# Pieces of the identity turned into an unread bank in nine waits of TensorE

## The chip, the cores and the metric

One Trainium2 chip, one of its cores. The metric is device time in microseconds for one execution of the whole program, lower is better. A profiled execution also gives the span from the first to the last instruction, and the clock that TensorE was granted, as a share of its full speed: 1.00 is 2.4 GHz, 0.50 is 1.2 GHz.

## The reference

A transformer block on x of 16 batches x 224 tokens x 512 channels, with 16 heads of 32 channels, and a context of 750 tokens per batch. Cut to what matters:

```python
shift_a, scale_a, gate_a, shift_m, scale_m, gate_m = split(silu(c) @ W_mod + b_mod, 6)
q, k, v = heads(modulate(ln(x), shift_a, scale_a) @ W_qkv + b_qkv)
x = x + gate_a * (softmax(q @ k.T * scale) @ v @ W_proj + b_proj)      # self attention
q_c = heads(ln(x) @ W_qc + b_qc)
k_c, v_c = heads(ln(context) @ W_kvc + b_kvc)
x = x + softmax(q_c @ k_c.T * scale) @ v_c @ W_cproj + b_cproj         # cross attention
h = gelu(modulate(ln(x), shift_m, scale_m) @ W_mlp1 + b_mlp1)          # MLP
x = x + gate_m * (h @ W_mlp2 + b_mlp2)
```

All in float32. The kernel splits most operands into a high and a low part and makes a product of three matmuls (the helper `product`, lines 72 to 74).

## The kernel before, in words

There are three phases: self attention (to about 767 us), cross attention (from 771 to about 1912 us) and the MLP (to the end). The places where one phase runs into the next are called seams. Self attention ends with a barrier of all engines (`clear`, lines 98 and 99); cross attention and the MLP are one program.

Self and cross attention go through the batches in *bodies*, one for a batch, of 16 *steps* (`h`), one for a head. TensorE's order is written out by hand in each body: `score` makes the scores of the next head (L599 in self, L1779 in cross), VectorE takes their maximum (`row_max`, L908; L1965 and L1967 in cross), after every fourth head TensorE turns the maxima into a row (`turn_maxima`, L616; L1767), VectorE splits that row (`split_maxima`, L915; L2012) and SyncE's queue copies it into the stacked queries (`place_maxima`, L437; L1669). Six steps later `score_t` makes the same scores with keys on the partitions and the maxima subtracted (L628; L1793), and ScalarE takes the exponential (L1160; L2138). Every four heads `pv` multiplies by the values (L645; in the last cross body `product_parts`, L1835) and `sums` adds up the probabilities (L652) that GpSimd has added in pairs (L1295). VectorE divides (`normalize`: reciprocal L922, product L925; L2019, L2025).

In between, `fill` puts projections of other batches into the steps (L72 to L74). In the last bodies there is less left to fill in. What the change touches or what follows on it there:

- Self attention's last full body (b.c = 15) runs from about 664 us. Step 2 has `score` of head 3, then `pv` and `sums` of the batch before. Step 3 fills in query channels ("c"), then turns maxima. Steps 4 and 5 turn x after its layernorm (`turn_y`, L562), of which the second waits for VectorE's `low_y` (L865). Step 6 has `pv` of the batch before, step 7 a fill of channels and then `turn_maxima`, which needs `row_max` of head 7. VectorE has the context's statistics (`stats_context`, L876) ahead of that maximum.
- The end of self attention is a last fill ("c", 1, 1), then the barrier.
- Cross attention begins with `score` of batch 0. SyncE's queue begins after the barrier too: it stores the last queries, loads and stacks (L1654, L1661), and then places the first maxima (L1669), for which `score_t` of step 6 waits.
- Cross attention's last body (b.c = 15) runs from about 1823 us. In step 6 the last products of the batch before let SyncE's queue load the first attention outputs (`load_first_o`, L1684, into mlp_o_raw). ScalarE splits them from step 8 on (`first_high_o`, L2113), between its exponentials. Steps 11 to 14 have the output projection of four tiles (`first_cproj`, L72 to L74 with mlp_wcp); that of tile 3 waits until VectorE has read tile 1 out of the same bank (`first_residual`, L1978).

A wait on a semaphore stops all that TensorE has behind it. The bank a step writes to is 512 words wide; the new function writes to columns 448 to 511, which nobody reads in the banks it is given.

Of the kernel before, what the change touches and what calls it, by code (L numbers as in the profile page):

```python
# [21 lines left out]
B, N, H = 16, 224, 512  # L22
# [54 lines left out]
def keep_warm(pe, bank, ident, count):  # L77

    for _ in range(count):
        pe.transpose(bank[:, 0:P], ident[:], ident[:])  # L80


def alloc(nc, ctx, phase):
# [80 lines left out]
def self_phase(nc, x, cond_t, w_mod, b_mod, w_qkv, b_qkv_t, w_proj, b_proj, w_qc, b_qc_t, gates, x1, qc, mod_t,  # L164
# [3 lines left out]
    with ExitStack() as ctx:  # L168
# [240 lines left out]
        def late_group(b, h, att, prv):  # L409

            if h % HPG != (LAG + HPG) % HPG:
                return []
            g = (h - LAG - HPG) // HPG
            if g >= 0:
                return [(b, g)] if att else []
            return [(b.plus(-1), g + KC)] if prv else []
# [139 lines left out]
        def _(pe):  # L556
# [185 lines left out]
            def body(b, att, nxt, prv, old):  # L742
                for h in range(NH):
                    for o, l in late(b, h, att, prv):
                        score_t(o, l)
                    work = fills(b, h, "kqvpc")
                    for f in work[0:1]:
                        fill(b, *f)
                    if h % HPG == HPG - 1 and att:
                        turn_maxima(b, h // HPG, old)  # L750
                    if h < NH - 1 and att:
                        score(b, h + 1)
                    if h == NH - 1 and nxt:
                        score(b.plus(1), 0)
                    for f in work[1:]:
                        fill(b, *f)

                    if seam_step(b, h) in V_AT:
                        cross_v(V_AT[seam_step(b, h)])
                    if seam_step(b, h) in K_AT:  # L760
                        cross_k(K_AT[seam_step(b, h)])
                    if b.c == 1 and h in (13, 14):
                        pe.wait_ge(proj_done, h - 12)
                        modulation_rows(h - 9)
                    for o, g in late_group(b, h, att, prv):
                        pv(o, g)
                        sums(o, g)
                    for _, c, _, o in fills(b, h, ("tx",)):
                        turn_x(b, c, o)
                    for t in TILES_AT.get(seam_step(b, h), ()):  # L770
                        turn_context(0, t)
                    for _, c, _, o in fills(b, h, ("ty",)):
                        turn_y(b, c, o, att)
                    if b.c == 0 and h == NH - 1:
                        pe.wait_ge(v_done, Batch(1).n(2, 2))
                        modulation_rows(3)
                    if b.c == 1 and h == 15:
                        pe.wait_ge(mlp_rows, 2)
                        turn_rows(pj_ps[1], lambda n, k: wm_mlp[0:B, n, 0, k * P:(k + 1) * P], mod_turned)
# [31 lines left out]
            turn_context(1, 5)  # L811
            fill(end, "c", 1, 0, last)
            fill(end, "c", 1, 1, last)

        @block.vector
        def _(dve):
# [620 lines left out]
def cross_phase(nc, ctx_in_dram, qc, o_dram, wkv, c_in, seam, pieces, ident, neg_half, eps, sems, banks, lead):  # L1437
# [291 lines left out]
    def tensor(pe):  # L1729
# [136 lines left out]
        def body(b, att, nxt, prv):  # L1866
            a = b.plus(1)
            for h in range(NH):
# [8 lines left out]
                for f, o in fill_at(b, h, "kv"):  # L1877
                    fill_(o, f, (0,))
                if cproj_due is not None:
                    first_cproj(cproj_due, (0,))  # L1880
                for o, l in late(b, h, att, prv):
                    score_t(o, l, 1)
                if h < NH - 1 and att:
                    score(b, h + 1, 0)
                if h == NH - 1 and nxt:
# [6 lines left out]
                    product_parts(*MID_PARTS[step])  # L1892
                if h % HPG == HPG - 1 and att:
                    turn_maxima(b, h // HPG)
                for o, l in late(b, h, att, prv):
                    score_t(o, l, 2)
                for u in (1, 2):
# [875 lines left out]
```

## Time and profile before

| | |
|---|---|
| median of 3 runs | 2616.03 us |
| lowest and highest | 2615.39, 2621.15 us |
| the profiled execution's own time | 2619.34 us |
| its span | 2617.5 us |
| mean granted clock | 0.991 |
| TensorE matmuls busy | 2578.0 us, 98% of the span |
| VectorE, ScalarE, GpSimd busy | 1694.1, 1126.6, 1275.6 us |

The profiled execution is one run of the same program. Its time has 1.8 us outside the span. TensorE's busy time counts a matmul from its start to its modelled end, about 0.2 us behind the moment at which the next one can start.

### The profile page before, as it was taken

Reading aid. Unit: us, or ns where it says so; the run is one execution under the profiler, and the core shown is the slowest. Engines: PE = TensorE matmul, PEld = TensorE weight load, DVE = VectorE, ACT = ScalarE, POOL = GpSimd, SP = SyncE. Lnnn points to the kernel's source line nnn. Section 1 sums busy time; section 2 is a strip of 40 time slices with the busy share of each in tenths; the row PEclk is TensorE's granted clock in tenths of the full one; section 3 lists DMA queues with packets and bytes.
Section 4 is the critical chain, followed back from the end, with each engine's and each line's share of the span. In section 5 each row is a group of like instructions: output and inputs, shape, how many; then the busy total and the mean of one; then the engine's idle time right before and its main releaser. Section 6 shows DMA issues by size and latency. Waiting matters only on the chain.

```text
span 2617.5 us, 50236 instructions
## 1 busy us (share of the span) xinstructions
PE 2578.0 (98%) x18696; PEld 2133.6 (82%) x18696; DVE 1694.1 (65%) x3399; ACT 1126.6 (43%) x2192; POOL 1275.6 (49%) x1426
## 2 busy tenths in 40 slices
PE   8999999999999999999999999999899999999999
PEld 6688888888788888888888888887678888888887
DVE  6677777777757777777777777776764444444442
ACT  4354454444535555555555555554552221212111
POOL 1445455454436777777777777775421121220230
PEclk9999999999899999999999999999899999999999
DMA  8454545555454444444444444434521111111110
GB/s 225 128 136 125 135 120 130 129 129 132 137 148 111 115 115 112 113 114 112 117 114 116 119 113 115 121 90 102 153 94 45 37 44 34 45 49 37 45 53 17
DMA packets 193045, 269.89 MB, mean 103 GB/s; under 512 B 34788, under 2 KB 112612, under 8 KB 192788
## 3 DMA queue, kind: packets, MB, share of 16 engines
q1 hardware_dynamic: 187116, 254.16, 36.9%
q0 software_dynamic: 3264, 7.92, 0.9%
q10 hardware_dynamic: 2424, 4.61, 0.7%
q8 instruction: 150, 2.46, 0.4%
q14 instruction: 91, 0.75, 0.1%
HBM read 111.11 MB, written 36.77 MB: 56 GB/s over the span
## 4 chain that ended last, share of the span: by engine, by line
PE 69%; DVE 1%; issue 0%; DMA 0%; ACT 0%; SPq 0%; DVEq 0%; ACTq 0%
PE late_tr_ps L1793 7%; PE late_sc_ps L1779 7%; PE late_or_ps L1806 5%; PE late_even_ps L72 5%; PE late_sc_ps L72 5%; PE late_even_ps L73 5%; PE late_even_ps L74 5%; PE late_sc_ps L74 5%; PE late_sc_ps L73 5%; PE late_odd_ps L72 3%; PE late_odd_ps L74 3%; PE late_odd_ps L73 3%; PE late_tr_ps L74 2%; PE late_tr_ps L72 2%; PE late_tr_ps L73 2%; PE late_odd_ps L1740 1%
## 5 line engine op out<-in xcount | busy, mean ns | idle before, releaser
L2138 ACT ACTIVATE cross_prT<-late_tr_ps 125x448 f32<-125x448 f32 x759 | 403.0, 544 | 273.5 <-PE late_tr_ps L1793 264.6
L1965 DVE TENSOR_REDUCE cross_parts<-late_sc_ps 112x1 f32<-112x500 f32 x512 | 335.5, 663 | 221.8 <-PE late_sc_ps L1779 220.7
L2211 POOL TENSOR_TENSOR cross_part<-cross_prT 125x448 f32<-125x448 f32 x232 | 271.2, 1169 | 214.6 <-ACT cross_prT L2138 176.9
L1295 POOL TENSOR_TENSOR self_psum<-self_prT 112x224 f32<-112x224 f32 x256 | 179.0, 699 | 328.3 <-ACT self_prT L1160 319.5
L1793 PE MATMUL late_tr_ps<-cross_qst,cross_kst 98*125 98x224 f32 x1536 | 309.5, 284 | 5.4 <-ACT cross_prT L2138 4.4
L1793 PEld LDWEIGHTS late_tr_ps<-cross_qst,cross_kst 98*125 98x125 f32 x1536 | 255.3, 188 | 55.8 <-ACT cross_prT L2138 16.5
L2613 ACT ACTIVATE mlp_hv<-late_sc_ps,mlp_b 128x512 f32<-128x512 f32 x112 | 77.0, 687 | 511.5 <-PE late_sc_ps L74 497.1
L2213 POOL TENSOR_TENSOR cross_part<-cross_part,cross_prT 125x448 f32<-125x448 f32 x232 | 268.5, 1157 | 18.2
L1779 PE MATMUL late_sc_ps<-cross_kst,cross_qst 96*112 96x500 f32 (+1 forms) x1024 | 262.2, 337 | 5.2 <-PEq L99 3.3
L2527 DVE CAST mlp_hT_h<-mlp_hv 128x512 fp32r<-128x512 f32 x112 | 55.9, 499 | 301.8 <-ACT mlp_hv L2613 301.8
L1160 ACT ACTIVATE self_prT<-self_st_ps 112x448 f32<-112x448 f32 x256 | 138.4, 541 | 167.6 <-PE self_st_ps L628 166.4
L1779 PEld LDWEIGHTS late_sc_ps<-cross_kst,cross_qst 96*112 96x112 f32 x1024 | 165.2, 179 | 20.1 <-issue 3.5
L908 DVE TENSOR_REDUCE self_nmax<-self_sc_ps 112x2 f32<-112x448 f32 x256 | 154.5, 614 | 33.3 <-PE self_sc_ps L599 33.2
L72 PE MATMUL late_sc_ps<-mlp_xT_l,mlp_w_h 128*128 128x512 f32 x448 | 175.8, 393 | 0.0
L74 PE MATMUL late_sc_ps<-mlp_xT_h,mlp_w_h 128*128 128x512 f32 x448 | 175.2, 391 | 0.0
L73 PE MATMUL late_sc_ps<-mlp_xT_h,mlp_w_l 128*128 128x512 f32 x448 | 175.0, 391 | 0.0
L1967 DVE TENSOR_REDUCE cross_parts<-late_sc_ps 112x2 f32<-112x500 f32 x256 | 170.2, 665 | 0.0
L2215 POOL TENSOR_TENSOR cross_psum<-cross_part 125x224 f32<-125x224 f32 x232 | 155.6, 671 | 18.2
L1806 PE MATMUL late_or_ps<-cross_prT,cross_vt 125*32 125x224 f32 x2784 | 143.7, 354 | 0.0
L72 PE MATMUL self_pj_ps<-self_xT_l,self_wqkv_h 128*128 128x224 f32 x512 | 140.6, 275 | 2.4 <-DVE self_wm_gates L1009 1.4
L74 PE MATMUL self_pj_ps<-self_xT_h,self_wqkv_h 128*128 128x224 f32 x512 | 140.6, 275 | 0.0
L73 PE MATMUL self_pj_ps<-self_xT_h,self_wqkv_l 128*128 128x224 f32 x512 | 140.3, 274 | 0.0
(343 smaller groups left out, 6870.9 us busy)
## 6 DMA issues: line engine op xcount, KB each, us to landing
cross_kst<-cross_nat_h SPq DMA_DIRECT2D x508, 93.8 KB, 2.2
cross_kst<-cross_nat_l SPq DMA_DIRECT2D x254, 93.8 KB, 2.2
cross_qst<-qc SPq DMA_DIRECT2D x192, 112.0 KB, 2.5
cross_c_in<-in_context SPq DMA_DIRECT2D x78, 224.0 KB
self_kst<-self_nat_h SPq DMA_DIRECT2D x128, 112.0 KB, 2.3
self_qst<-self_natq_h SPq DMA_DIRECT2D x128, 112.0 KB, 3.0
self_x_in<-in_x SPq DMA_DIRECT2D x16, 448.0 KB, 3.8
self_kst<-self_nat_l SPq DMA_DIRECT2D x64, 112.0 KB, 2.2
```

The source lines that it names most:

```text
L72: pe.matmul(out, lhs[0], rhs[1], start=first, stop=False)
L73: pe.matmul(out, lhs[1], rhs[0], start=False, stop=False)
L74: return pe.matmul(out, lhs[0], rhs[0], start=False, stop=last)
L1295: pool.tensor_tensor(psum[:, j], prT[:, j, 0], prT[:, j, 1], ALU.add).then_inc(p_summed, 1)
L1779: last = pe.matmul(sc_ps[u][0:QN, at:at + cn], qst[g][0:TERMS * HD, j, t * QN:(t + 1) * QN], kst[g][j][0:TERMS * HD, c0:c0 + cn], start=Tr ...
L1793: last = pe.matmul(bank(h, c)[0:SN, m * N:(m + 1) * N], kst[g][j][:, kt * SN:(kt + 1) * SN], qst[g][:, j, :], start=True, stop=True)
L1806: last = pe.matmul(or_ps[HD * j:HD * j + HD, 0:N], vt[b.par][:, kt, h * HD:h * HD + HD], prT[:, slot(h), kt], start=kt == 0, stop=kt == ST ...
L1965: dve.tensor_reduce(parts[:, g % 2, j, u, 0:1], sc_ps[u][0:QN, 0:SHALF[0]], AX_X, ALU.max, negate=True).then_inc(maxed, 1)
L1967: dve.tensor_reduce(parts[:, g % 2, j, :, 1], sc_ps[u][0:QN, 0:QT * SHALF[1]].rearrange("p (t k) -> p t k", t=QT), AX_X, ALU.max, negate=T ...
L2138: act.activation(probabilities(b, h)[:, 2 * c:2 * c + 2], bank(h, c)[0:SN, 0:2 * N].rearrange("p (k t) -> p k t", k=2), ACT.Exp).then_inc( ...
L2211: pool.tensor_tensor(part[:], prT[:, j, 0:2], prT[:, j, 2:4], ALU.add).then_inc(pre_summed, 1)
L2213: pool.tensor_tensor(part[:], part[:], prT[:, j, 4:6], ALU.add).then_inc(pre_summed, 1)
```

## The change

A function `stay_busy` transposes half of the identity (64 of its rows, 128 columns wide, against a 64 x 64 identity) into columns 448 to 511 of a bank, so and so many times. It is called in nine places; four of them have a wait of their own ahead of it, so that the bank is not being read by another engine.

```diff
+def stay_busy(pe, bank, ident, count):
+    for _ in range(count):
+        pe.transpose(bank[:, 448:512], ident[0:64, :], ident[0:64, 0:64])
...  self attention, body (b.c = 15)
                         turn_maxima(b, h // HPG, old)
+                    if b.c == B - 1 and h == 2:
+                        pe.wait_ge(m_row, b.n(KC, 0))
+                        stay_busy(pe, tx_ps, ident, 16)
                     if h < NH - 1 and att:
                         score(b, h + 1)
...
                     for o, g in late_group(b, h, att, prv):
+                        if b.c == B - 1 and h == 6:
+                            stay_busy(pe, pj_ps[1], ident, 16)
                         pv(o, g)
+                        if b.c == B - 1 and h == 2:
+                            stay_busy(pe, tx_ps, ident, 18)
                         sums(o, g)
+                    if b.c == B - 1 and h == 5:
+                        pe.wait_ge(c_l, Batch(B - 4).n(2, 2))
+                        stay_busy(pe, pj_ps[1], ident, 10)
...  end of self attention
             fill(end, "c", 1, 1, last)
+            stay_busy(pe, tx_ps, ident, 40)
...  cross attention, body (step = h in the last body)
                 if cproj_due is not None:
+                    if step == 14:
+                        pe.wait_ge(maxed, b.n(NH * 3, (NH - 1) * 3 - 2))
+                        stay_busy(pe, sc_ps[0], ident, 28)
                     first_cproj(cproj_due, (0,))
                 for o, l in late(b, h, att, prv):
                     score_t(o, l, 1)
+                if step == 5:
+                    pe.wait_ge(*turn_bank_free(b, 1))
+                    stay_busy(pe, odd_ps, ident, 12)
                 if h < NH - 1 and att:
                     score(b, h + 1, 0)
...
+                if step in (8, 9):
+                    pe.wait_ge(m_row, b.n(KC, 2))
+                    stay_busy(pe, odd_ps, ident, {8: 12, 9: 28}[step])
                 for o, l in late(b, h, att, prv):
                     score_t(o, l, 2)
```

In all 180 transposes. Nothing is removed or reordered.

## Rows read from the trace of the kernel before

**Rows 1.** The page: TensorE's granted clock in 40 slices, in tenths.

```profile
PEclk9999999999899999999999999999899999999999
```

**Rows 2.** Stretches (us): busy PE, PEld, DVE, ACT, POOL; granted clock, DMA share, GB/s.

```profile
671.33:678.16 6.83, 5.93 (x34) 5.19 (x34) 1.75 (x6) 2.88 (x6) 2.32 (x4) 0.50 0.93 224
681.57:688.40 6.83, 6.62 (x44) 5.21 (x45) 6.67 (x21) 1.46 (x3) 2.03 (x3) 0.50 0.64 193
770.32:777.15 6.83, 6.30 (x20) 5.90 (x21) 2.72 (x6) 0.52 (x1) 3.59 (x6) 0.50 1.04 299
1842.11:1845.52 3.41, 3.41 (x36) 1.75 (x38) 1.63 (x3) 0.98 (x2) 2.14 (x5) 0.50 0.84 233
1855.76:1862.59 6.83, 5.05 (x38) 3.46 (x42) 4.65 (x8) 3.72 (x7) 1.54 (x2) 0.50 0.60 181
1883.07:1886.48 3.41, 3.41 (x11) 2.67 (x9) 3.38 (x6) 0.54 (x1) 3.03 (x3) 0.50 0.01 2
1844.00:1855.50 11.50, 10.61 (x119) 6.72 (x111) 6.12 (x12) 5.54 (x11) 5.26 (x5) 0.93 1.05 273
```

**Rows 3.** Timeline of PE, transposes of 16 columns (start, us, engine, idle in brackets).

```profile
17.56 0.66 PE L739 MATMUL self_st_ps<-shared_ident,self_bm 16*128 16x16 f32 x8
```

**Rows 4.** Timeline of PE, self attention's last full body.

```profile
669.49 0.46 PE L599 MATMUL self_sc_ps<-self_kst,self_qst 96*112 96x224 f32 x2 [1.09 <-DVE self_nmax L908]
...
672.23 0.98 PE L652 MATMUL self_or_ps<-self_psum,self_ones 112*32 112x224 f32 x8 [1.39 <-POOL self_psum L1295]
...
676.21 0.39 PE L616 MATMUL self_tx_ps<-shared_ident,self_nmax 112*8 112x112 f32 x1
...
679.72 0.61 PE L562 MATMUL self_tx_ps<-shared_ident,self_x_res 112*128 112x112 f32 x4 [0.59 <-DVE self_yT_l L865]
...
681.77 1.72 PE L645 MATMUL self_or_ps<-self_prT,self_vt 112*32 112x224 f32 x16 [1.03 <-DVE self_ou L925]
...
687.37 0.35 PE L616 MATMUL self_tx_ps<-shared_ident,self_nmax 112*8 112x112 f32 x1
...
704.86 0.62 PE L701 MATMUL self_pj_ps<-shared_ident,cross_c_in 125*128 125x125 f32 x4 [1.54 <-DVE self_y L856]
```

**Rows 5.** Timeline of DVE, same stretch, and its last work before the barrier.

```profile
676.63 0.26 DVE L915 CAST self_mrow_h<-self_tx_ps 8x112 fp32r<-8x112 f32 x1 [4.97 <-PE self_tx_ps L616]
...
686.72 0.59 DVE L908 TENSOR_REDUCE self_nmax<-self_sc_ps 112x2 f32<-112x448 f32 x1
...
768.41 0.81 DVE L846 SCALAR_TENSOR_TENSOR self_natq_l<-self_pj_ps,self_bqcs,self_natq_h 128x224 fp32r<-128x224 f32 x2 [1.63 <-ACT self_natq_h L1146]
```

**Rows 6.** Timeline of PE, the first seam and cross attention's step 6.

```profile
770.85 1.56 PE L1779 MATMUL late_sc_ps<-cross_kst,cross_qst 96*112 96x500 f32 x4 [3.30 <-PEq L99]
...
792.10 0.60 PE L1793 MATMUL late_tr_ps<-cross_qst,cross_kst 98*125 98x224 f32 x4
```

**Rows 7.** Timeline of SyncE's queue and, last row, PE: maxima placed by DMA.

```profile
789.47 0.65 SPq L1669 DMA_DIRECT2D cross_qst<-cross_mrow_l  x1
...
68.49 0.67 SPq L437 DMA_DIRECT2D self_qst<-self_mrow_l  x1
...
70.30 0.50 PE L628 MATMUL self_st_ps<-self_qst,self_kst 98*112 98x224 f32 x2 [0.17 <-DMA self_qst<-self_mrow_l]
```

**Rows 8.** Timeline of PE, four waits of cross attention's last body.

```profile
1839.99 0.48 PE L1779 MATMUL late_sc_ps<-cross_kst,cross_qst 96*112 96x500 f32 x1 [0.86 <-DVE cross_parts L1965]
...
1853.51 0.48 PE L1793 MATMUL late_tr_ps<-cross_qst,cross_kst 98*125 98x224 f32 x2 [0.76 <-ACT cross_prT L2138]
...
1857.54 0.76 PE L1793 MATMUL late_tr_ps<-cross_qst,cross_kst 98*125 98x224 f32 x2 [1.91 <-ACT cross_prT L2138]
...
1881.80 0.50 PE L72 MATMUL late_odd_ps<-mlp_wcp_l,mlp_xT_l 128*128 128x512 f32 x1 [1.78 <-DVE mlp_x L1978]
```

**Rows 9.** The chain that ended last, 1847 to 1857 us (start, us, what).

```profile
1847.54 8.71 DMA mlp_o_raw<-o_cross
```

**Rows 10.** Timeline of DVE ahead of the last wait.

```profile
1880.48 0.67 DVE L1965 TENSOR_REDUCE cross_parts<-late_sc_ps 112x1 f32<-112x500 f32 x1
```

## The prediction

> **What bounds the kernel now.** I read the page first. TensorE's matmuls are busy for 98% of the span (the table above), and its granted clock has two dips, in slices 11 and 29, which are the two seams [rows 1]. So the kernel is bound by TensorE, and what can be won in the seams is idle time and slow clock. The windows by stretch then show the dips as six stretches in which the clock stood at its lower level, 0.50, together 34.1 us (6.83 four times, 3.41 twice), with TensorE busy for 5.93, 6.62, 6.30, 3.41, 5.05 and 3.41 = 30.7 us of it [rows 2]. At full clock that work would take half, so 15.4 us is the most that a better clock can return. I call the stretches A to F in their order. Ahead of each the timeline shows TensorE idle: 1.09 and 1.39 us ahead of or into A, 0.59 and 1.03 ahead of B [rows 4], 3.30 ahead of C [rows 6], 0.86 ahead of D, 0.76 and the begin of 1.91 ahead of E, 1.78 ahead of F [rows 8]. The nine calls stand in just these waits. The reader should look next at who would be late if TensorE were faster after them: VectorE, SyncE's queue and a DMA, stretch by stretch.
>
> **What a transpose costs.** The trace has none of 64 columns. Eight of 16 columns take 0.66 us together with the last one's latency of about 0.2, so about 0.065 us each [rows 3]; four of 112 columns take 0.61, so about 0.11 each at the most [rows 4]. Those are the bounds. If the cost goes with the columns, 64 would take 0.06, and the small ones show a floor of 0.065, so I take 0.065; at the lower clock twice the 0.06, about 0.11.
>
> **Do they fit the waits?** At 0.065: 16 are 1.04 us against 1.09 idle, 18 are 1.17 against 1.39, 10 are 0.65 against 0.59, 16 are 1.04 against 1.03 [rows 4]; 12 are 0.78 against 0.86, 12 are 0.78 against 0.76, 28 are 1.82 against 1.91 [rows 8]. A further 0.2 us of matmul latency lies ahead of each idle time and hides the small excess. These seven cost nothing; without that cover the 112 transposes would be 7.3 us. The waits put ahead of three of them ask for rows of maxima, channels or a bank that were done long before, so nothing queues behind them. Two do not fit.
>
> The 40 at the end of self attention are 2.6 us. TensorE's last product ends at 767.55 (770.85 less 3.30), its stream 0.2 us earlier, so TensorE would end at about 770.1 with the latency, while VectorE, now the last to come to the barrier, ends at 769.22 [rows 5, 6]. The barrier, and with it all engines, comes 0.8 us later (0.6 at 0.06 each, 2.6 at 0.11).
>
> The 28 in step 14 must first wait for `row_max` of head 14, which VectorE runs from 1880.48 to 1881.15 [rows 10], late, just ahead of the read that releases TensorE at 1881.80 [rows 8]. So they run from 1881.15 to about 1883.0, and the projection behind them starts 1.2 us later than now (1.0 at 0.06 each, 2.4 at 0.11).
>
> **What the full clock returns, if the falls go away.**
> - A. From 672.23 to the turned maxima at 676.21 TensorE works without a wait [rows 4]; 4.0 us become 2.0. From there VectorE is busy without a break from 676.63 to past 687 (6.67 of 6.83 us in B's row) [rows 2, 5], so everything behind it moves by these 2.0 and no more. Return 2.0, at most 3.0.
> - B. TensorE now reaches the next turned maxima at 687.37, and VectorE ends the maximum that it needs at 687.31 [rows 4, 5]. A faster TensorE only waits there. Only the last 1.0 us of B returns 0.5. At most 3.3.
> - C. TensorE would come to step 6, now at 792.10 [rows 6], up to 3.1 us earlier. But `score_t` needs the maxima, whose DMA SyncE's queue issues at 789.47 after a row of copies that starts at the barrier; the same kind of DMA elsewhere released TensorE 1.8 us after its issue (68.49 to 70.30) [rows 7]. So it can start at 791.3, and with the later barrier at 792.1. Delay and clock cancel: 0.0, between 1.8 lost (a barrier 2.6 later) and 0.2 won (0.6 later).
> - D. The products of step 6 stand in the chain, but what follows is a DMA of 8.71 us [rows 9], in a stretch in which the DMA engines are full (share 1.05 from 1844 to 1855.5) [rows 2]. Issued earlier it lands hardly earlier, so the 1.7 us are waited away in step 9. I take 0, at most 1.7.
> - E. It follows that landing; 5.05 us busy give up to 2.5, ScalarE's exponentials between them take a little: 2.3.
> - F. All TensorE: 1.7 returned, 1.2 spent on the late transposes: 0.5.
>
> The sum is 2.0 + 0.5 + 0.0 + 0.0 + 2.3 + 0.5 = 5.3 us. The profiled execution's own time is 2619.34 (span 2617.5 and 1.8 around it), so 2614.0. It was 3.3 us above the median of 2616.03. A run near the median may have lacked one of the low stretches, and what it lacks can't be taken out of it; so I don't subtract the whole 5.3 there. I forecast 2613.5 for the median, 2.5 us or 0.1% better. About 0.2%, 5.2 us, is what a measurement of this kernel can tell from no change, so this counts as no change.
>
> **A rule that speaks against it.** TensorE idles 1.54 us at 704.86 between transposes [rows 4], and the clock stays at 1.00 there (the next low stretch is C [rows 2]), while the idle 1.78 us ahead of F, among matmuls, is followed by 0.50 [rows 2, 8]. The Trainium skill, TensorE: Matmul & The Clock Gate, Part 4 (PE-mode transpose), says that a transpose "doesn't count as PE-busy the same way". The two waits lean against that rule, but do not settle it; by the rule the sum would be that of the third rival below.
>
> **Rivals.**
> 1. *It all passes through.* VectorE, the queue and the DMA make room, since their work starts earlier too: 15.4 less 0.8 and 1.2 is 13.4 us, 2606. Against it stand the three meeting points above, of which that in B is within 0.1 us.
> 2. *The waits that open drop the clock again*, the slower side. At full clock TensorE comes to the maxima of step 7 2.6 us before VectorE (5.6 us of work from 681.77 become 2.9, then VectorE), and 2.3 us early to step 6 of cross attention (3.1 less 0.8). Neither wait has transposes, and idle times of 1.8 and 1.9 us were enough for a fall before. In step 9 D's 1.5 us lengthen a wait whose 28 transposes stay the same. A fall costs half of 3.4 or 6.8 us, so 1.7 to 3.4, twice, and E's 2.3 are not won: 2614.0 + 3.4 to 6.8 + 2.3 = 2619.7 to 2623.1. It is decided where the idle rest passes about 1.8 us, and by how the wait falls in time.
> 3. *Transposes don't hold the clock.* All six low stretches stay, the 28 in step 9 run mostly at 0.11 each and overrun by 0.9 us, with 0.8 for the barrier and 1.2 in step 14: 2.9 us more, 2622.
>
> **How the numbers follow.** The forecast 0.45 (its own range 2610 to 2617.5), the first rival 0.20, the second 0.20, the third 0.10, something between them 0.05. Under 2610.8 lie the first rival and a fifth of the forecast: faster 0.30. Over 2621.3 lie half of the second and most of the third, less what a median near the lower runs takes off: slower 0.15. No change 0.55. The range that leaves out 2 in 10 is 2607 to 2621.5.
>
> **What would show it.** In the profile after: spacing of the new transposes near 0.065 us; the clock at 1.00 where A, C and F stood; the first matmul of cross attention 3.4 to 3.5 us after the last product of self attention becomes 4.2 to 4.4; an idle time of some 2.6 us at the turned maxima of step 7 and of some 2 us at the `score_t` of step 6, with or without low clock behind; the DMA into mlp_o_raw landing at the same distance from the seam; the projection of tile 3 about 1.9 us behind `row_max` of head 14. The prediction is wrong if VectorE or SyncE's queue turn out to have slack, or if the new waits drop the clock in each run.

## The result, and the profile after

The changed kernel takes 2620.57 us in the median of 13 runs (2616.95 to 2623.29), the kernel before 2615.39 us in the median of 13 (2612.52 to 2621.15) beside it. The ratio is 1.0015 with a 95% interval of 1.0008 to 1.0022, so it is slower, by 0.15%. The forecast was 2613.5, faster by 0.1%; the time lies in the range from 2607 to 2621.5, the direction does not.

The two profiled executions hide this: before's own time is 2619.34 us, after's 2619.05. They were unlike draws, one 3 to 4 us above its median, the other 1.5 below it. So these profiles can't be subtracted from each other; they can be followed place by place.

The windows of the profile after, in the columns of [rows 2]. The first, third and fourth rows lie where A, C and D stood, the others are its own low stretches and the time ahead of the last:

```profile
669.00:675.83 6.83, 6.49 (x73) 4.99 (x71) 2.99 (x9) 4.13 (x8) 4.21 (x6) 1.00 0.72 184
680.26:687.09 6.83, 6.83 (x48) 5.25 (x47) 5.69 (x19) 0.54 (x1) 2.98 (x4) 0.50 0.47 152
770.32:777.15 6.83, 6.75 (x39) 6.50 (x40) 5.42 (x10) 1.15 (x2) 4.88 (x8) 1.00 0.83 247
1842.11:1845.52 3.41, 3.41 (x65) 2.21 (x61) 1.43 (x3) 1.57 (x3) 1.07 (x2) 1.00 1.03 263
1854.45:1861.28 6.83, 6.06 (x42) 3.83 (x46) 3.82 (x6) 2.84 (x6) 2.42 (x2) 0.50 0.82 246
1878.35:1881.76 3.41, 2.23 (x30) 2.12 (x30) 3.33 (x8) 2.11 (x4) 1.09 (x3) 1.00 0.01 4
1881.76:1885.17 3.41, 3.41 (x10) 2.74 (x10) 1.62 (x3) 0.54 (x1) 2.70 (x3) 0.50 0.00 0
```

Three stretches are gone (A, C, D) and three remain in new places, at 680.26 for B, 1854.45 for E, 1881.76 for F: 17.1 us of half clock instead of 34.1. Had these 17 us returned half of themselves, the span would be some 8 us shorter. It is 0.2 us shorter.

The timeline of PE of the changed kernel, lines with L86 being the new transposes (start, us, engine; idle in brackets):

```profile
669.03 0.47 PE L605 MATMUL self_sc_ps<-self_kst,self_qst 96*112 96x224 f32 x2
...
673.92 0.26 PE L622 MATMUL self_tx_ps<-shared_ident,self_nmax 112*8 112x112 f32 x1
...
676.72 0.84 PE L86 MATMUL self_pj_ps<-shared_ident 64*128 64x64 f32 x10
...
679.28 1.30 PE L86 MATMUL self_pj_ps<-shared_ident 64*128 64x64 f32 x16
680.51 1.72 PE L651 MATMUL self_or_ps<-self_prT,self_vt 112*32 112x224 f32 x16
...
685.98 0.39 PE L622 MATMUL self_tx_ps<-shared_ident,self_nmax 112*8 112x112 f32 x1
...
766.07 2.74 PE L86 MATMUL self_tx_ps<-shared_ident 64*128 64x64 f32 x40
770.40 0.91 PE L1796 MATMUL late_sc_ps<-cross_kst,cross_qst 96*112 96x500 f32 x4 [1.59 <-PEq L105]
...
790.16 0.67 PE L1810 MATMUL late_tr_ps<-cross_qst,cross_kst 98*125 98x224 f32 x4 [1.20 <-DMA cross_qst<-cross_mrow_l]
...
1837.95 0.48 PE L1796 MATMUL late_sc_ps<-cross_kst,cross_qst 96*112 96x500 f32 x1
...
1849.91 0.48 PE L1810 MATMUL late_tr_ps<-cross_qst,cross_kst 98*125 98x224 f32 x2
...
1851.91 1.98 PE L86 MATMUL late_odd_ps<-shared_ident 64*128 64x64 f32 x28
1854.78 0.76 PE L1810 MATMUL late_tr_ps<-cross_qst,cross_kst 98*125 98x224 f32 x2 [0.89 <-ACT cross_prT L2164]
...
1856.82 1.18 PE L1810 MATMUL late_tr_ps<-cross_qst,cross_kst 98*125 98x224 f32 x4 [0.45 <-DMA cross_qst<-cross_mrow_l]
...
1862.17 0.48 PE L1810 MATMUL late_tr_ps<-cross_qst,cross_kst 98*125 98x224 f32 x2
...
1879.57 1.98 PE L86 MATMUL late_sc_ps<-shared_ident 64*128 64x64 f32 x28 [1.18 <-DVE cross_parts L1991]
1881.48 0.57 PE L72 MATMUL late_odd_ps<-mlp_wcp_l,mlp_xT_l 128*128 128x512 f32 x1
```

Set each line against its twin of before. The difference of the two start times is how far after is ahead, and its steps are the ledger:

| place | before | after | ahead | step |
|---|---|---|---|---|
| scores ahead of A [rows 4] | 669.49 | 669.03 | 0.46 | |
| maxima turned, through A [rows 4] | 676.21 | 673.92 | 2.29 | +1.8 |
| maxima turned, through B [rows 4] | 687.37 | 685.98 | 1.39 | -0.9 |
| cross attention begins [rows 6] | 770.85 | 770.40 | 0.45 | -0.9 |
| `score_t`, step 6 [rows 6] | 792.10 | 790.16 | 1.94 | +1.5 |
| ahead of D [rows 8] | 1839.99 | 1837.95 | 2.04 | +0.1 |
| `score_t`, step 8, past D [rows 8] | 1853.51 | 1849.91 | 3.60 | +1.6 |
| `score_t`, step 9 [rows 8] | 1857.54 | 1854.78 | 2.76 | -0.8 |
| step 11, past E | 1863.81 | 1862.17 | 1.64 | -1.1 |
| projection of tile 3 [rows 8] | 1881.80 | 1881.48 | 0.32 | -1.3 |

In this pair of executions, what was won in A, the first seam and D (4.9 us) was lost in B, at the barrier, in step 9, E and step 14 (5.0 us). The experiments ask which of the two columns belongs to the change.

### The profile page after: what moved, and what is told of

Read it like the earlier page. It is cut to its first block, busy times and chain, and to the rows that moved or that the text cites. A ratio compares the mean times of both kernels' runs of the same rounds, so it can differ in the third digit from the quotient of the medians.

```text
span 2617.3 us, 50596 instructions
## 1 busy us (share of the span) xinstructions
PE 2583.7 (99%) x18876; PEld 2140.2 (82%) x18876; DVE 1694.0 (65%) x3399; ACT 1126.6 (43%) x2192; POOL 1276.2 (49%) x1426
## 4 chain that ended last, share of the span: by engine, by line
PE 68%; SPq 1%; DVE 1%; issue 0%; DMA 0%; ACT 0%; DVEq 0%
PE late_tr_ps L1810 7%; PE late_sc_ps L1796 6%; PE late_or_ps L1823 5%; PE late_sc_ps L72 5%; PE late_sc_ps L74 5%; PE late_sc_ps L73 5%; PE late_even_ps L72 5%; PE late_even_ps L73 5%; PE late_even_ps L74 5%; PE late_odd_ps L72 3%; PE late_odd_ps L74 3%; PE late_odd_ps L73 3%; PE late_tr_ps L74 2%; PE late_tr_ps L72 2%; PE late_tr_ps L73 2%; PE late_odd_ps L1757 1%
## 5 line engine op out<-in xcount | busy, mean ns | idle before, releaser
L2239 POOL TENSOR_TENSOR cross_part<-cross_part,cross_prT 125x448 f32<-125x448 f32 x232 | 268.7, 1158 | 18.2
L2241 POOL TENSOR_TENSOR cross_psum<-cross_part 125x224 f32<-125x224 f32 x232 | 155.5, 670 | 18.2
```

The costliest lines, as they stand in the source:

```text
L2239: pool.tensor_tensor(part[:], part[:], prT[:, j, 4:6], ALU.add).then_inc(pre_summed, 1)
```

## The experiments

Each kernel ran 11 times unless said otherwise, and the kernel before beside it. "Mean" is over these runs, the granted clock too. A mean clock below 1 is read as half clock: 0.9938 over 2615 us is 32 us of it.

### The kernel before, again

No edit.

> The kernel before once more, with no edit, so that the clock and span of each of its runs are seen. Theory 1 (the profiled execution is typical in its clock): the granted clock is 0.990 to 0.992 in most runs, the median lies at 2615 to 2616, and a new profile shows the same six stretches of half clock in the two seams, 37 us in all, within 0.2 us of their places. Theory 2 (the profiled execution of before, 3.3 us above its median, had more half clock than most): most runs show 0.993 or more, and the new profile lacks at least one of the six stretches; then part of what the change took away was not there to take.

Median 2617.15 us, ratio 1.0003 (0.9994 to 1.0013), clocks from 0.993 to 0.997. The profiled execution took 2613.39 us at 0.995. Its timeline has no low stretch at A or F, 3.41 us in place of B's 6.83, and 3.41 us more at 701.63, where the first profile has none; windows of it:

```profile
660.00:677.70 17.70, 12.45 (x104) 9.77 (x101) 13.19 (x29) 8.21 (x16) 8.08 (x11) 1.00 0.55 142
677.74:681.15 3.41, 3.41 (x31) 1.81 (x29) 3.41 (x7) 0.60 (x2) 0.66 (x1) 0.50 1.04 313
701.63:705.04 3.41, 3.41 (x31) 2.23 (x24) 2.94 (x6) 1.32 (x3) 3.25 (x3) 0.50 0.24 70
766.48:773.31 6.83, 5.61 (x18) 5.32 (x19) 2.61 (x5) 0.00 (x0) 3.06 (x5) 0.50 1.05 288
1838.27:1841.68 3.41, 3.41 (x27) 2.21 (x31) 2.23 (x4) 0.98 (x2) 2.65 (x6) 0.50 0.85 227
1851.92:1858.75 6.83, 6.83 (x51) 4.08 (x55) 4.93 (x9) 2.89 (x6) 2.99 (x3) 0.50 0.78 236
1880.00:1912.00 32.00, 29.59 (x344) 20.28 (x346) 20.70 (x51) 18.79 (x35) 6.84 (x10) 1.00 0.31 106
```

That is 23.9 us in the seams, where the first profile has 34.1. The same program has its low stretches for other lengths, and in part at other places, from one execution to the next. Theory 2 holds. Four profiles are of kernels that fill no wait at all (the two of before, and `waits_only` and `before_w_later` below). A and F are in one of them. B, C, D and E are in all four, B twice and C once at half length. Over the 149 runs of the kernel before that stood beside the experiments the clock goes from 0.990 to 0.998 with a mean of 0.9938; the profiled execution of the forecast had 0.991, and only six of the 149 are as low. The time goes with the clock: the 19 runs at 0.992 or less took 2619.5 us in the mean, the 43 at 0.993 2617.6, the 35 at 0.994 2615.9, and the 52 at 0.995 or more 2614.6.

### Parts of the change, alone

`self_body`, `end_40`, `steps_5_8_9` and `step_14` each keep one group of calls. As an example, the calls that `self_body` leaves out:

```diff
-            stay_busy(pe, tx_ps, ident, 40)
...
-                    if step == 14:
-                        pe.wait_ge(maxed, b.n(NH * 3, (NH - 1) * 3 - 2))
-                        stay_busy(pe, sc_ps[0], ident, 28)
...
-                if step == 5:
-                    pe.wait_ge(*turn_bank_free(b, 1))
-                    stay_busy(pe, odd_ps, ident, 12)
...
-                if step in (8, 9):
-                    pe.wait_ge(m_row, b.n(KC, 2))
-                    stay_busy(pe, odd_ps, ident, {8: 12, 9: 28}[step])
```

> Only the four calls in self attention's last full body (16, 18, 10 and 16 transposes), the other calls left out. Theory 1 (the sum of the forecast: the clock stays up where the waits are filled): 2.5 us under before, no half clock between 665 and 695. Theory 2 (what the profile of the changed kernel shows in this place is the rule: one fall of the two goes, the other stays, a clock period earlier): about 1 us under before, one stretch of 6.8 us that begins near 680.3, and stretch C at 770 unchanged. Theory 3 (the calls cost time in places that the profile doesn't show): 1 us or more over before, with the same clock as in theory 2.

> Only the 40 transposes at the end of self attention. Theory 1 (forecast: the barrier comes 0.8 us later, what stretch C returns is lost to the wait for m_in's maxima): 0.8 us over before, no half clock at 770. Theory 2 (stretch C's 1.6 us come back, and the wait for the maxima at step 6 takes 1.2 of them): 0.4 us under before to 0.4 over it. Theory 3 (the later barrier puts everything behind it at another place against the DMA queues): 2 us or more over before, in a profile whose cross bodies wait more often than before's.

> Only the calls of the last cross body's steps 5, 8 and 9 (12, 12 and 28 transposes). Theory 1 (forecast: stretch E goes and returns 2.3 us): 2.3 us under before, no half clock from 1850 to 1870. Theory 2 (the changed kernel's profile is the rule: the stretch of 3.4 at 1842 goes, the one of 6.8 stays a period earlier): within 0.5 us of before, one stretch of 6.8 us near 1854.5 to 1856. Theory 3 (no cover: the transposes' own time is on the path): 1 us or more over before.

> Only the 28 transposes of the last cross body's step 14. Theory 1 (they wait for the last heads' maxima and then take 1.98 us, where before's wait of 1.78 us was for mlp_x alone): about 1.4 us over before, a row of 28 transposes that starts after an idle time near 1.2 us, and the wait that before shows at this place lengthened from 1.78 to 3.2 us. Theory 2 (the loss of this place lies behind the wait as well, in head 15's exponentials, which come late): 2 us or more over before. Theory 3 (the clock that they hold pays for them): within 0.7 us of before, and no half clock behind 1880.

| | median us | ratio to before, interval | mean clock |
|---|---|---|---|
| `self_body` | 2616.76 | 1.0002 (0.9994 to 1.0011) | 0.9941 |
| `end_40` | 2618.61 | 1.0006 (0.9997 to 1.0015) | 0.9940 |
| `steps_5_8_9` | 2616.33 | 0.9995 (0.9986 to 1.0004) | 0.9955 |
| `step_14` | 2618.70 | 1.0004 (0.9996 to 1.0013) | 0.9930 |

No part is told from before by its time alone. `self_body` was to be 2.5 us under, and its interval, 1.6 us under to 2.9 over, rules that out. `steps_5_8_9` was to be 2.3 us under, and its interval, 3.7 us under to 1.0 over, does not. The latter's profile has what theory 2 said, a stretch of 6.83 us at 1856.01, and one of 3.41 at 1838.94 besides. `self_body` fits none of its three theories whole: its stretch begins where theory 2 has it, but there is none at 770, and its time is not below before's. The profiles say more, since a stretch between two fixed instructions can be read to 0.02 us.

*Self attention's last body.* From one turning of maxima to the next ([rows 4]: 676.21 to 687.37, 11.16 us) the 13 profiles without narrow transposes there (seven with empty waits, six with the wide pieces of the kernels below) took 11.11 to 11.16 us, and the six with them 12.06, 12.16, 12.55, 12.68, 12.89 and 13.92. The first of the two turnings settles stretch A: from the turning ahead of it to 676.21 before took 12.12 us, and all 18 others, with and without the calls, 10.3. Stretch A was in that one execution, and the 16 and 18 transposes of step 2 cost nothing. In the second half the low stretch of B is there at full length, 6.83 us, in all six with narrow transposes, in four of the seven with empty waits (twice at half length, once not at all), and in none of the six with wide pieces. (Of the 20 profiles `matmul_fill`, below, is left out here, since its fills overran the waits.)

Why the calls cost there is seen in two profiles with the same length of half clock in that half. `steps_5_8_9` has no transposes in this body; its window, and PE's timeline:

```profile
678.41:685.24 6.83, 6.53 (x42) 4.58 (x43) 6.68 (x14) 1.99 (x4) 0.66 (x1) 0.50 0.92 284
```

```profile
674.97 0.26 PE L622 MATMUL self_tx_ps<-shared_ident,self_nmax 112*8 112x112 f32 x1
...
680.73 1.72 PE L651 MATMUL self_or_ps<-self_prT,self_vt 112*32 112x224 f32 x16
...
686.09 0.26 PE L622 MATMUL self_tx_ps<-shared_ident,self_nmax 112*8 112x112 f32 x1 [0.17 <-DVE self_nmax L914]
```

VectorE is busy for 6.68 of 6.83 us, TensorE still waits 0.17 us for it at the end, and the 11.12 us are those of full clock: the waits that were left empty had absorbed 6.83 us of half clock. (`wide_transposes`, below, has no low clock there and takes 11.12 us too, with a wait of 1.18 us for VectorE at the end.) `self_body` has such a fall at 679.92, and filled waits:

```profile
679.86 1.95 PE L86 MATMUL self_pj_ps<-shared_ident 64*128 64x64 f32 x16
681.74 1.72 PE L651 MATMUL self_or_ps<-self_prT,self_vt 112*32 112x224 f32 x16
...
687.00 0.26 PE L622 MATMUL self_tx_ps<-shared_ident,self_nmax 112*8 112x112 f32 x1
```

The 16 take 1.88 us to the next start, 0.118 each, against 0.065 at full clock. The products begin 7.29 us after the first turning, against 5.76 in `steps_5_8_9`, and the next turning comes after 12.55 us with no wait ahead of it. A second thing goes into this stretch: TensorE waits there for the row of maxima that SyncE's queue copies (self_qst<-self_mrow_l), 0.56 to 0.75 us in the four shorter of the six, 1.06 us in that of 12.89 (`no_40_no_14`) and 2.17 us in that of 13.92 (`no_40_14_w_later`). With empty waits even 1.45 us of it, beside 3.41 us of half clock (`before_again`), left the 11.12 us as they were. So the upper end of the six is also that wait's, which filled waits no longer hide.

*The end of self attention.* From the end of the last product to cross attention's first matmul the changed kernel takes 770.40 less 766.13 = 4.27 us against 3.30 [rows 6]: 0.97 more. From there to the `score_t` of step 6, profiles without the 40 took 20.9 to 21.3 us with a fall of 6.8 us there, 19.9 to 20.2 with one of 3.4, and 19.2 in the one without a fall; the four with them took 19.8 to 20.0, with a fall of 3.4 in three of them. The six profiles in which no wait ahead of this place is filled and the 40 are left out average 20.7 us, the four with the 40 transposes 19.9. So the 40 cost 0.97 and give back about as much, 0.85, by few profiles. `end_40` has its stretch at 768.03, and its waits elsewhere are those of before, so its profile bears out theory 2; its median does not contradict theory 1.

*Step 14.* The row at 1879.57 above waits for a maximum (1.18 us), then 1.91 us go by before the projection starts, where before waited 1.78 us in all [rows 8]: 1.3 us. `step_14` shows the same two numbers, 1.18 and 2.08 us. The fall that the calls were to prevent came under them or right behind them in three of the four profiles with these calls (1881.76 in the changed kernel, 1879.71 in `step_14`, 1876.8 in `after_w_later`, below), and not in `after_again`. Of the 13 profiles with this wait empty four have it, within 1.4 us behind the projection's start: the first of before and three of the kernels with wide pieces in seven waits. Theory 1 holds for the place; the mean, 1.5 us over before, is not outside the interval.

### The changed kernel again, without its two costly places, and with its waits alone

`no_40_no_14` leaves out the 40 and the 28 of step 14. `waits_only` keeps the five added `wait_ge` (the description of the change counts four; its diff has five, and six of the nine calls stand behind one) and makes `stay_busy` empty.

> The changed kernel once more, on the chip of the three below. Theory 1 (the loss is the kernel's own: its clock is a little higher than before's, and its waits longer): 3 to 6 us over before, a mean granted clock of 0.994 to 0.995 against 0.9938 over 33 runs of before. Theory 2 (the first comparison drew an unlucky spread): within 2 us of before.

> The changed kernel without the 40 at the end of self attention and without the 28 of step 14. Theory 1 (these two are the loss: 1.0 and 1.4 us): 2.4 us or more under the changed kernel of this call, within 2 us of before. Theory 2 (the loss is that of waits for transfers, which take what the clock returns, wherever the calls are): within 1 us of the changed kernel.

> The changed kernel with its four added waits and without any transpose. Theory 1 (the time is in the transposes; the waits are for work that had come): as before, within 0.5 us, and a mean clock of 0.9935 as before. Theory 2 (the wait for the last heads' maxima itself delays mlp_o's product in step 14): 1 us or more over before, with the idle time of that place near 1.8 us or above.

`after_again`: median 2618.36 us in 12 runs, ratio 1.0004 (0.9996 to 1.0012), mean clock 0.9950. By its time this is theory 2, within 2 us of before, by its clock theory 1, and taken alone it is not told from before. Over all 25 runs of the changed kernel the mean is 2619.3 us at a clock of 0.9948, against 2616.4 at 0.9938 over the 149 of before; in the first measurement the means are 4.3 us apart, in the second 1.3. So the loss is nearer 3 us than 5, and it comes with a little less half clock (27 us instead of 32). `no_40_no_14`: 2616.31 us, ratio 0.9998 (0.9989 to 1.0006), 2 us under `after_again` in the median: near theory 1's 2.4. `waits_only`: 2617.22, ratio 1.0000 (0.9991 to 1.0009), clock 0.9939, an idle time of 1.83 us in step 14: the waits cost nothing, the transposes do.

### What is put into the waits

Three kernels keep the nine places and change the filling.

```diff
-    for _ in range(count):
-        pe.transpose(bank[:, 448:512], ident[0:64, :], ident[0:64, 0:64])
+    # matmul_fill
+    for _ in range(round(count * 0.6)):
+        pe.matmul(bank[:, 448:512], ident[0:64, :], ident[0:64, 0:64], start=True, stop=True)
+    # wide_transposes
+    for _ in range(round(count * 0.6)):
+        pe.transpose(bank[:, 384:512], ident[:], ident[:])
+    # wide_matmuls
+    for _ in range(round(count * 0.25)):
+        pe.matmul(bank[:, 384:512], ident[:], ident[:], start=True, stop=True)
```

> The changed kernel with plain matmuls of the same pieces in place of the transposes, 0.6 times as many because a plain fp32 matmul of 64 columns should take about 0.11 us, so the waits are filled for about as long. Theory 1 (transposes count for the clock as matmuls do): clocks and time as those of the changed kernel, within 0.0005 and 1.5 us. Theory 2 (transposes count for little: the array is idle through much of them): a mean clock above 0.9955, at most two stretches of half clock in the seams, and 1 to 3 us under the changed kernel.

> The nine waits filled with transposes of the whole 128x128 identity, 0.6 times as many (about 0.11 us each in keep_warm's burst at the start), so the same waits are filled for the same time and each transpose moves twice the columns. Theory 1 (the pieces of 64 columns are too small to count, wide ones count): mean clock 0.9955 or more, no stretch of 6.8 us begins between 679 and 681 and none near 1854 to 1859, and at least 1.5 us under the changed kernel's mean. Theory 2 (no transpose counts): mean clock 0.994 to 0.995, the stretch near 680.5 stays, time within 1.5 us of the changed kernel.

> The same waits filled with plain fp32 matmuls of the whole identity, a quarter as many (0.2 to 0.3 us each, worked out from the 0.24 us that one of 64 columns took). Theory 1 (plain matmuls count where transposes don't): mean clock 0.9955 or more and no half clock in the filled places, while the wide transposes show 0.995 or less. Theory 2 (what is put into the waits doesn't decide, since the waits at other places are enough for a fall): clock and time as the changed kernel's.

`matmul_fill` (5 runs): 2640.62 us, ratio 1.0086 (1.0073 to 1.01), clock 0.990. Its size was misjudged: a plain fp32 matmul of 64 columns took 0.24 us, not 0.11, so the fills overran their waits by some 20 us in all. It still shows the one thing that it was for. PE's timeline at the end of self attention, and windows of it:

```profile
770.34 6.47 PE L86 MATMUL self_tx_ps<-shared_ident 64*128 64x64 f32 x48
```

```profile
771.40:774.80 3.40, 3.40 (x33) 3.40 (x33) 0.67 (x2) 0.00 (x0) 0.00 (x0) 1.00 1.03 247
774.80:778.20 3.40, 2.01 (x10) 1.82 (x9) 0.00 (x0) 0.00 (x0) 0.00 (x0) 0.50 0.03 5
```

TensorE is busy from 770.34 to 776.81 without a break, all of it narrow plain matmuls, and the clock falls in the middle, at 774.8. So a busy row of narrow pieces did not hold the clock, and it is not the transposing.

Wide pieces mostly do hold it. `wide_transposes`: mean clock 0.9980, `wide_matmuls` 0.9976, 10 to 13 us of half clock left. In its profile `wide_transposes` has one low stretch in both seams:

```profile
660.00:800.00 140.00, 131.63 (x952) 113.86 (x951) 98.67 (x205) 65.69 (x127) 58.52 (x70) 1.00 0.50 138
1800.00:1854.00 54.00, 50.54 (x469) 37.15 (x468) 35.78 (x63) 26.30 (x52) 19.14 (x23) 1.00 0.59 152
1854.01:1860.84 6.83, 6.13 (x51) 3.47 (x53) 3.08 (x5) 2.13 (x4) 3.32 (x3) 0.50 0.77 228
1860.90:1912.00 51.10, 47.52 (x483) 35.05 (x476) 36.41 (x76) 28.93 (x54) 16.38 (x21) 1.00 0.31 103
```

Theory 1 of `wide_transposes` holds for the mean clock, and its mean time, 2615.7 us, is 3.6 us under the changed kernel's 2619.3; only the stretch at 1854.01 is against it. Theory 1 of `wide_matmuls`, by which plain matmuls count where transposes don't, is refuted, since both held the clock. Against the kernel before, the time is hardly better: 2616.03 us, ratio 0.9996 (0.9987 to 1.0005), and 2615.65, ratio 0.9996 (0.9988 to 1.0005). Twenty microseconds less half clock bought 1 us or less. (These pieces have more rows and more columns than the narrow ones; which of the two counts was not tried.)

Step 9 of `wide_transposes` shows where part of the rest went. Timelines of PE and ACT:

```profile
1853.60 0.48 PE L1810 MATMUL late_tr_ps<-cross_qst,cross_kst 98*125 98x224 f32 x2 [2.01 <-ACT cross_prT L2164]
...
1855.57 1.18 PE L1810 MATMUL late_tr_ps<-cross_qst,cross_kst 98*125 98x224 f32 x4 [0.70 <-DMA cross_qst<-cross_mrow_l]
```

```profile
1852.39 0.72 ACT L2139 ACTIVATE mlp_xT_l<-mlp_o_raw,mlp_bv 128x512 fp32r<-128x512 f32 x1 [3.72 <-DMA mlp_o_raw<-o_cross]
```

and the chain of waits:

```profile
1847.73 7.79 DMA cross_qst<-cross_mrow_l
```

There are two waits. In the longer one, 2.01 us, TensorE waits for ScalarE's exponentials, and ScalarE has stood 3.72 us ahead of them, in `first_high_o`, until the load of mlp_o_raw landed. The shorter, 0.70 us, is for the row of maxima of 3.5 KB, which took 7.79 us from SyncE's queue to its landing. In the changed kernel the two are 0.89 us (ScalarE waits 2.60 us for mlp_o_raw) and 0.45 us (a row of 6.53 us, issued at 1850.25, TensorE goes on at 1856.82). Ahead of the row are seven weight pieces and the four of mlp_o_raw, 256 KB each; ahead of mlp_o_raw are the seven pieces. The issues of mlp_o_raw, in `wide_matmuls`, where TensorE comes there earliest (SyncE's queue issues them at 1839.35, that of before at 1846.68, and the last landed 8.71 us after 1847.54 [rows 9]):

```profile
mlp_o_raw<-o_cross SPq DMA_DIRECT2D x4, 256.0 KB, 12.0
```

and in the kernel before, again:

```profile
mlp_o_raw<-o_cross SPq DMA_DIRECT2D x4, 256.0 KB, 6.3
```

What counts is how soon mlp_o_raw follows the pieces. With all seven ahead of it, the eight profiles that issue it 6.5 to 6.9 us behind the first weight load (mlp_wcp_raw) show 9.1 to 12.0 us to its landing (the median of the four transfers), the six that issue it 8.3 to 9.6 us behind show 6.0 to 9.6. Without D's half clock TensorE is at the products of step 6 sooner, and so the load is issued sooner. In `wide_matmuls` ScalarE waits 6.06 us for it, and the idle time of step 9 is 4.65 us. This is no matter of the fills alone: `self_body`, with nothing filled in cross attention, has no D either, and waits 3.61 us.

### Fewer transfers ahead of mlp_o_raw and the row

```diff
-                    load_pieces({2: range(0, 7), 3: range(7, 14), 0: range(14, len(pieces)), 1: ()}[g])
+                    load_pieces({2: range(0, 4), 3: range(4, 14), 0: range(14, len(pieces)), 1: ()}[g])
```

Three weight pieces are issued behind the row of step 9's maxima instead of ahead of it and of mlp_o_raw: `before_w_later`, `after_w_later`, `no_40_14_w_later` (the changed kernel's own transposes in seven waits), and `wide_no_40_14_w_later` with its repetition `wide_again` (wide matmuls in the same seven). `wide_matmuls_no_40_no_14` has the wide matmuls without the move, `wide_no_40_14_o_later` moves `load_first_o` behind the row instead.

> The plain wide matmuls, without those at the end of self attention and in step 14, which cost about 1.0 and 1.3 us in the profiles. Theory 1 (fills that count hold the clock in the seams and the two costly places are gone): 2 to 4 us under before. Theory 2 (no fill holds it): within 1 us of before.

> The kernel before with three weight pieces (256 KB each) issued behind the maxima's row of step 9 instead of ahead of it. Theory 1 (the transfers ahead of the row set when it lands): mlp_o_raw lands in 6 us or less after its issue, the idle time ahead of step 9's scores is under 0.8 us, and the mean lies 0.5 to 2 us under before. Theory 2 (the wait is the exponentials' or the row's own path): the idle time stays and the time is within 0.5 us of before.

> The changed kernel with the same three pieces issued later. Theory 1: the waits of 0.9 and 0.45 us behind the 28 transposes of step 9 go, and the mean is 1 to 3 us under the changed kernel's 2618.5 to 2620.0. Theory 2 (what the changed kernel loses is only its 40 and its 28 of step 14): within 0.7 us of it.

> Plain wide matmuls in seven waits, none at the end of self attention and in step 14, and the three pieces later. Theory 1 (clock held and the transfers out of the way, so that the return comes through): a mean of 2612 to 2614, 3 to 5 us under before. Theory 2 (the return is taken elsewhere, or the fill costs as much): 2615 or more, as without the move.

> The same fill with mlp_o_raw's four loads issued behind the maxima's row instead of the three pieces. Theory 1 (any megabyte out from ahead of the row frees it): no idle time over 0.8 us ahead of step 9's scores, but mlp_o's cast then waits for its own load, so that its first product comes later: 2613 to 2616. Theory 2: the idle time of step 9 stays at 1.5 us or more.

> The changed kernel's own pieces of 64 columns in seven waits, none at the end of self attention and in step 14, three weight pieces later. Theory 1 (the width decides: only wide fills hold the clock): mean clock 0.995 to 0.9955, a mean time 1.5 us or more over that of the wide fill in this call. Theory 2 (the width doesn't matter to the time): within 1 us of the wide fill.

> Plain wide matmuls in seven waits with three pieces later, once more. Theory 1 (its gain is real): 2 to 4.5 us under before, mean clock 0.9965 to 0.998. Theory 2 (the first measurement was a lucky draw): within 1 us of before.

| filling | pieces where they were | three pieces later |
|---|---|---|
| none | 2616.26, median of 149 | 2616.34, ratio 1.0001 (0.9992 to 1.0010) |
| narrow, nine waits | 1.0015 (1.0008 to 1.0022) and 1.0004 (0.9996 to 1.0012) | 2615.98, 1.0000 (0.9991 to 1.0008) |
| narrow, seven waits | 2616.31, 0.9998 (0.9989 to 1.0006) | 2612.60, 0.9987 (0.9978 to 0.9996) |
| wide, seven waits | 2615.25, 0.9996 (0.9987 to 1.0004) | 2612.63, 0.9990 (0.9981 to 0.9999); again 2611.67, 0.9984 (0.9975 to 0.9993) |

The move alone does nothing to the time. In `before_w_later` mlp_o_raw lands after 4.1 us and nothing waits in step 9, as theory 1 says, and the time is that of theory 2. Why is open: the second profile of before had no idle time in step 9 to win either, but its first, `step_14` and `waits_only`, which fill nothing up to there, had 1.91, 1.72 and 1.79 us. With filled waits the move is worth about 3 us in each row. In `after_w_later` the 28 transposes of step 9 are followed by `score_t` without a wait, mlp_o_raw lands after 5.5 us (4.7 to 8.6 in the three kernels of the last rows; only at 8.6 are there still waits, of 0.72 and 0.73 us):

```profile
1851.72 1.97 PE L86 MATMUL late_odd_ps<-shared_ident 64*128 64x64 f32 x28
1853.62 0.48 PE L1810 MATMUL late_tr_ps<-cross_qst,cross_kst 98*125 98x224 f32 x2
```

From the products of step 6 to those of step 10 the four kernels with narrow transposes in steps 8 and 9 and early pieces took 17.7 to 19.4 us, the two with late pieces 15.1 and 15.8. Moving mlp_o_raw instead gives 2616.19 us (0.9999, 0.9991 to 1.0008) and an idle time of 2.60 us in step 9, as theory 2 of `wide_no_40_14_o_later` has it. Its cause is the one that theory 1 named:

```profile
1854.69 0.72 ACT L2134 ACTIVATE mlp_xT_l<-mlp_o_raw,mlp_bv 128x512 fp32r<-128x512 f32 x1 [4.01 <-DMA mlp_o_raw<-o_cross]
```

The load is issued only at 1849.56, and ScalarE waits 4.01 us for it ahead of the exponentials. So mlp_o_raw has to land early, and it is the weight pieces ahead of it that have to go.

The last rows beat the kernel before by 0.10 to 0.16%. The width adds little to them: theory 2 of `no_40_14_w_later` (0.3 to 0.7 us by the means). The clocks are close too, 0.9961 with the narrow pieces and 0.9968 and 0.9965 with the wide ones, so there the narrow ones do not lag as they do in nine waits (0.9948 against 0.9980). `wide_matmuls_no_40_no_14` lies between its theories, 1.3 us under before by the means where 2 to 4 were expected of a held clock.

## Why the prediction was wrong

- *What bounds the kernel.* The six stretches were taken for the kernel's own. A and F were largely one execution's: A came in 1 of 20 profiles, F in 1 of the 4 that fill nothing. So A's 2.0 and F's 1.7 were mostly not there to win. The forecast said that a run near the median may lack one of them and took 2.8 us off for it; the mean run had 32 us of half clock, the profiled one 47.
- *What a transpose costs.* 0.065 at full clock was right (28 in 1.98 us, 0.22 of it latency), and about 0.11 at half clock was measured as 0.118.
- *What the full clock returns, if the falls go away*, and *These seven cost nothing*: **this is where the prediction failed.** The falls of B and E did not go away under the narrow transposes; in the changed kernel both stood again at full length (680.26 and 1854.45), where 0.5 and 2.3 us were to be won. And the transposes fit their waits only at full clock: under half clock they take nearly twice as long (0.118 against 0.065 us) and use up the idle time that hid the fall. In self attention's last body this cost 0.9 us or more in six profiles of six (11.1 us became 12.06 to 13.92), where 2.0 for A and 0.5 for B were to be won.
- *The 40*: 0.8 forecast, 0.97 measured, and what goes with C's fall about cancels it (0.85), as forecast.
- *The 28 of step 14*: 1.2 forecast, 1.3 measured. F's return of 1.7 did not come: most executions have no F, and with the calls a fall came in three of four profiles.
- *D*: 1.6 were won, and step 9 took 0.8 of them back; the forecast had nothing left. *E* was to return 2.3 behind it and returned nothing: the clock fell again, and there were the waits for mlp_o_raw and then for the row. The landing of mlp_o_raw was named as what TensorE would meet. That it takes the longer the sooner it follows the weight pieces (9.2 us against 8.3 in this pair) was not seen.
- *The rivals.* The third was nearest: the fills don't hold the clock, and the 40 and the 28 are paid, 2622. Its reason was half wrong. The Trainium skill, TensorE: Matmul & The Clock Gate, Part 4 (PE-mode transpose), has that a transpose "doesn't count as PE-busy the same way". Here wide transposes kept the mean clock at 0.998 and narrow plain matmuls fell at 774.8, so this case does not bear the rule out. Of the second rival the wait at `score_t` of step 6 came, 1.20 us instead of 2, with no fall behind it. The first was refuted even with the clock at 0.998, which brought 1 us or less and not 13.4.

Put together for a typical run: 0.9 to 1.5 us in self attention's body (the two profiles of the changed kernel and `self_body`), 1.2 from step 6 to step 10 (18.3 against 17.1 us in the means of four and of six profiles), 1.3 at step 14 and nothing net at the barrier. That is 3.4 to 4.0 us, against 2.9 as the difference of the means over all runs. The terms are read from few profiles each (the six of step 6 to 10 without narrow transposes go from 15.4 to 18.2 us), and `self_body` and `steps_5_8_9` alone are not told from before, so this division is an estimate; that the whole is slower is measured in the first comparison, and that the seven waits with later pieces are faster in three. Of the share of the clock and that of the later pieces in that gain, only the second was measured apart (about 3 us). What stays open besides is the spread between the two measurements of the changed kernel, 1.0015 and 1.0004, and why the landing of mlp_o_raw varies by microseconds at nearly the same distance: 6.0 to 9.6 us in five profiles that issue it 8.3 to 9.3 us behind the first weight load.

## What to carry to other kernels

Profile the kernel before more than once before a low clock in it is counted as winnable, and read the granted clock of all runs: what a fall costs depends on the idle time around it, which may hide it whole. Filling a wait takes that cover away, so a fill that doesn't hold the clock has to be paid for (0.9 us or more in self attention's last body), and any fill must end before the wait does under the low clock too. Then ask what the time that is won runs into: here a load that queues behind seven pieces of 256 KB and that ScalarE waits for ahead of TensorE's exponentials, and behind it a 3.5 KB row. Only both edits together gained.

## What had not been expected of the hardware

Narrow matmuls, 64 rows and 64 columns, kept TensorE busy for 4.4 us without a gap before the clock fell under them, while wide transposes of 128 columns that filled the same waits for the same time took the mean clock from 0.9938 to 0.998, and narrow transposes to 0.9948. A plain fp32 matmul of 64 columns took 0.24 us where a transpose of the same size took 0.065. And one transfer of 3.5 KB took 5.5 to 7.8 us behind eleven of 256 KB from the same queue, in the four profiles in which TensorE waited for it.
